# Ten of 22 row groups multiplied by h at once on VectorE and summed row by row on ScalarE

## The reference

```python
indices = jnp.take_along_axis(all_indices, pk, axis=-1)
de = down_embed[indices]
ue = up_embed[indices]
z = jnp.einsum('btd,bthkd->bthk', h, de)
z = act(z * jax.nn.softmax(sc, axis=-1))          # act is silu
out = jnp.einsum('bthk,bthkd->btd', z, ue)
```

## Time and profile before

| | |
|---|---|
| median of 3 runs | 3196.2 us |
| lowest and highest | 3188.67 and 3196.66 us |
| span of the profiled execution, first to last instruction | 3168.2 us |
| VectorE busy | 2783.2 us, 88% |
| TensorE busy (matmuls) | 2818.4 us, 89% |
| ScalarE busy | 2105.8 us, 66% |
| POOL busy | 2098.0 us, 66% |
| DMA bytes moved | 856.45 MB |

### The profile page before, as it was taken

How to read it: one execution, slowest core, us unless ns; L and a number is a source line. 1 busy time by engine, 2 the same in 40 slices (tenths; PEclk the granted TensorE clock), 3 DMA queues, 4 the chain that set the end, 5 groups by cost and what they waited for, 6 DMA issues and landing times.

```text
span 3168.2 us, 39919 instructions
## 1 busy us (share of the span) xinstructions
PE 2818.4 (89%) x9216; PEld 1501.1 (47%) x9216; DVE 2783.2 (88%) x10160; ACT 2105.8 (66%) x6641; POOL 2098.0 (66%) x2056
## 2 busy tenths in 40 slices
PE   7998999999899999999999999899899999998963
PEld 4444455545454545444445444444445454444431
DVE  3488999999989899999999899898999999898987
ACT  4476766767776667776666677666676666677642
POOL 0067666677667677666667767667766666766676
PEclk9999999999999999999999999999999999999986
DMA  8078888888888788888888888888888888888888
GB/s 289 16 265 277 276 270 269 274 283 289 275 270 267 261 282 293 279 281 269 269 275 300 263 277 280 265 268 291 270 278 275 271 275 290 282 279 275 269 296 280
DMA packets 189837, 856.45 MB, mean 270 GB/s; under 512 B 36192, under 2 KB 39392, under 8 KB 189088
## 3 DMA queue, kind: packets, MB, share of 16 engines
q0 software_dynamic: 163840, 805.44, 76.5%
q1 hardware_dynamic: 19104, 34.87, 3.2%
q10 hardware_dynamic: 6656, 13.60, 1.2%
HBM read 845.38 MB, written 8.39 MB: 269 GB/s over the span
## 4 chain that ended last, share of the span: by engine, by line
PE 57%; POOL 11%; DVE 10%; DMA 10%; ACT 6%; issue 6%; SPq 0%; DVEq 0%; ACTq 0%; POOLq 0%
PE bank L465 14%; POOL ring L279 11%; DMA ring<-embed,idx 10%; PE bank L508 8%; PE bank L362 7%; PE bank L481 6%; PE bank L342 5%; DVE bank L1166 4%; PE bank L496 4%; PE bank L444 3%; PE bank L371 3%; ACT xc L691 3%; DVE ring L1152 2%; PE bank L472 2%; ACT raw L688 1%
## 5 line engine op out<-in xcount | busy, mean ns | idle before, releaser
L279 POOL DMA_INDIRECT ring<-embed,idx x2048 | 2096.7, 1024 | 1057.9 <-issue 544.3
L1166 DVE SCALAR_TENSOR_TENSOR bank<-ring,coef,bank 128x512 f32<-128x512 f32 x1312 | 990.8, 755 | 7.4 <-issue 0.2
L1152 DVE SCALAR_TENSOR_TENSOR ring<-ring,hcur 128x256 f32<-128x256 f32 x2048 | 827.1, 423 | 185.7 <-DMA ring<-embed,idx 182.6
L508 PE MATMUL bank<-ring,diag_c 128*128 128x512 f32 x1344 | 668.8, 628 | 119.6 <-ACT diag_c L666 103.9
L657 ACT ACTIVATE coef<-prob,zp 128x1 f32<-128x1 f32 x2048 | 459.1, 293 | 456.1 <-DVE ring L1152 454.9
L465 PE MATMUL bank<-w_up,zs 128*128 128x512 f32 x1024 | 490.4, 630 | 69.2 <-ACT zs L779 65.8
L508 PEld LDWEIGHTS bank<-ring,diag_c 128*128 128x128 f32 x1344 | 246.6, 199 | 385.8 <-issue 224.9
L465 PEld LDWEIGHTS bank<-w_up,zs 128*128 128x128 f32 x1024 | 200.7, 201 | 329.7 <-issue 238.6
L997 DVE SCALAR_TENSOR_TENSOR xc<-raw,taps,xc 128x128 f32<-128x128 f32 x960 | 266.0, 351 | 53.8 <-ACT xc L691 53.8
L342 PE MATMUL bank<-w_in,ut 128*128 128x512 f32 (+1 forms) x768 | 285.1, 524 | 4.4 <-ACT seg L679 4.3
L666 ACT ACTIVATE diag_c<-cst,coef 128x128 f32<-128x128 f32 x672 | 234.8, 394 | 49.4 <-PE bank L508 38.9
(11 more groups left out here) (147 smaller groups left out, 3685.1 us busy)
## 6 DMA issues: line engine op xcount, KB each, us to landing
ring<-embed,idx POOLq DMA_INDIRECT x2048, 4.6
ring<-uT SPq DMA_DIRECT2D x4, 2048.0 KB, 14.3
ut<-uT SPq DMA_DIRECT2D x32, 256.0 KB, 6.5
zs<-u SPq DMA_DIRECT2D x32, 256.0 KB, 5.7
out<-acc SPq DMA_DIRECT2D x32, 256.0 KB, 4.7
w_up<-W_upT ACTq DMA_DIRECT2D x1, 4096.0 KB, 12.7
w_in<-W_in ACTq DMA_DIRECT2D x1, 2560.0 KB, 17.0
w_in<-W_in ACTq DMA_DIRECT2D x1, 2048.0 KB, 21.5
```

Source lines behind the costliest of these rows:

```text
L279: pool.indirect_dma_start(out=ring[:, k % RING, :], out_offset=None, in_=embed, in_offset=bass.IndirectOffsetOnAxis(ap=idx[:, half, k:k + ...
L508: m = pe.matmul(bank[SUM][:, :], diag_c[:, (len(PE_ROWS) * t + n) % DIAGS, :], ring[:, k % RING, DP:ROW], start=(n == 0), stop=(n == len(P ...
L1152: m = dve.scalar_tensor_tensor(out=ring[:, k % RING, 0:DP], in0=ring[:, k % RING, 0:DP], scalar=1.0, in1=hcur[:, :], op0=ALU.mult, op1=ALU ...
L1166: dve.scalar_tensor_tensor(out=total if n == len(DVE_ROWS) - 1 else running[:, :], in0=ring[:, k % RING, DP:ROW], scalar=coef[:, k:k + 1], ...
```

## The change

In the ten groups 3, 5, 7, 8, 9, 10, 11, 13, 16 and 19 (`SUMMED`; five of three picks, five of four) VectorE no longer makes a dot for each pick. It waits until all picks of the group have landed and multiplies all of their first 256 numbers by h in one tensor_tensor (768 or 1024 elements), in place in the ring; the weighs of the group two before follow behind it. ScalarE then runs over each product with the probability as its scale and writes the sum of the scaled products to `zp` (a Copy with `accum_out`), waits for its last sum, and makes one silu for all columns of the group in place of one a pick. The other twelve groups stay as they are.

```diff
--- before.py
+++ after.py
@@ -67,6 +67,8 @@
 PE_GRPS = [g for g in range(NGRP) if "P" in GROUPS[g]]
 NPG = len(PE_GRPS)
 assert FIRST[NGRP] == PICKS and FIRST[NEW] < RING
+SUMMED = (3, 5, 7, 8, 9, 10, 11, 13, 16, 19)
+assert all(FIRST[g] % RING < (FIRST[g + 1] - 1) % RING for g in SUMMED)
 
 
 def signal_of(k):
@@ -209,6 +211,7 @@
         cur_ok, conv_ok, cbm_ok, xdt_ok, g_ok, xdec_ok, yoff_ok, y_half, y_ok, dcy_ok, st_ok, rr_ok, bn_ok, x1_ok, h_ok = (
             sem(n) for n in ("cur_ok", "conv_ok", "cbm_ok", "xdt_ok", "g_ok", "xdec_ok", "yoff_ok", "y_half", "y_ok",
                              "dcy_ok", "st_ok", "rr_ok", "bn_ok", "x1_ok", "h_ok"))
+        zp_ok = sem("zp_ok")
         top1_ok, found_ok, pair_ok, top2_ok, pick_ok, ixy_ok, idx_ok, soft_ok, dot_ok, row_used, sum_ok, r2_ok, o_ok = (
             sem(n) for n in ("top1_ok", "found_ok", "pair_ok", "top2_ok", "pick_ok", "ixy_ok", "idx_ok", "soft_ok", "dot_ok",
                              "row_used", "sum_ok", "r2_ok", "o_ok"))
@@ -653,8 +656,16 @@
                 if g == 0:
                     act.wait_ge(soft_ok, 4 * t + 4)
                 act.wait_ge(dot_ok, NGRP * t + g + 1)
-                for k in range(FIRST[g], FIRST[g + 1]):
-                    m = act.activation(coef[:, k:k + 1], prob_v[:, k:k + 1], ACT.Silu, scale=zp[:, k:k + 1])
+                if g in SUMMED:
+                    for k in range(FIRST[g], FIRST[g + 1]):
+                        m = act.activation(ring[:, k % RING, 0:DP], ring[:, k % RING, 0:DP], ACT.Copy,
+                                           scale=prob_v[:, k:k + 1], accum_out=zp[:, k:k + 1])
+                    m.then_inc(zp_ok, 1)
+                    act.wait_ge(zp_ok, len(SUMMED) * t + SUMMED.index(g) + 1)
+                    m = act.activation(coef[:, FIRST[g]:FIRST[g + 1]], zp[:, FIRST[g]:FIRST[g + 1]], ACT.Silu)
+                else:
+                    for k in range(FIRST[g], FIRST[g + 1]):
+                        m = act.activation(coef[:, k:k + 1], prob_v[:, k:k + 1], ACT.Silu, scale=zp[:, k:k + 1])
                 m.then_inc(coef_ok, 1)
                 mine = rows_of(g, "P")
                 if mine:
@@ -1154,6 +1165,14 @@
                 if last:
                     m.then_inc(dot_ok, 1)
 
+            def products(t, g):
+
+                lo, hi = FIRST[g], FIRST[g + 1]
+                for k in range(lo, hi):
+                    dve.wait_ge(row_in[k % RING], 16 * (uses(k) * t + k // RING + 1))
+                of = ring[:, lo % RING:lo % RING + hi - lo, 0:DP]
+                dve.tensor_tensor(of, of, hcur[:, :].unsqueeze(1).to_broadcast([P, hi - lo, DP]), ALU.mult).then_inc(dot_ok, 1)
+
             def weigh(t, k, first):
 
                 n = DVE_ROWS.index(k)
@@ -1183,8 +1202,10 @@
                 if g == 0:
                     dve.wait_ge(hcur_ok, t + 1)
                     dve.wait_ge(soft_ok, 4 * t + 4)
+                if g in SUMMED:
+                    products(t, g)
                 for n in range(max(len(mine), len(late))):
-                    if n < len(mine):
+                    if n < len(mine) and g not in SUMMED:
                         dot(t, mine[n], n == len(mine) - 1)
                     if n < len(late):
                         if n == 0:
```

## The result

The change makes the kernel slower: 3348.9 us (3344.9 to 3354.2, four runs) against 3194.4, a ratio of 1.0495 (95% interval 1.0476 to 1.0515). The span of the profiled execution grew from 3168.2 to 3343.1 us, by 174.9 us; that is more than the 154 of the medians, as the profiled execution before was quicker than the timed ones. The forecast was 3303, by 3.4 us a tile. From one profiled execution to the other the tile lost 5.0 us in the mean, and the end behind the last tile 20.

A forecast was written before the change was run, and what follows sets the result against it. The bound was taken as a chain through ScalarE ahead of the up projection, TensorE and gathers, not VectorE's queue. 0.2 + 1.4 + 1.0 + 0.8 = 3.4 us a tile, 105 us, plus 2, gave span 3275; with 28, 3303 (3190 to 3385).

The forecast's parts named there:

- The direction: Whole kernel: slower, chance 0.75, against 0.07 for the same and 0.18 for faster.
- (a): Group 3: its product waits for the third row and ScalarE's longer group uses up its wait; 0.2 us a tile.
- (b): Group 5 on ScalarE between the copies ahead of the up projection: nothing covers its sums; +1.40 us a tile.
- (d): Group 16: four sums ahead of four diagonals delay the gather needing its first row; +0.8 us a tile.
- (c): Groups 7 to 13: 7 to 11 free on ScalarE; blocking at 11 and 13 reaches TensorE's turns, 1.0 us a tile.
- the end: Groups after the last tile: some 2 us more in all.
- VectorE's gain: VectorE sheds 2.1 us a tile, 67 us over 32 tiles, into waits for rows; nothing subtracted from the forecast.
- VectorE's total work: Faster rival: VectorE's queue sets the pace, so 2.1 us a tile come off, 65 us, to 3131; chance 0.18.
- Only the front: Rival: only (a) and (b) count, with cheaper sums, some 1.3 us a tile, 40 us, to 3236; chance 0.16.
- The gathers: Rival: POOL's gathers starting under VectorE's products wait them out, net +2.4 us of POOL a tile; chance 0.13.

The follow-up runs named there:

- rowwise: The change with all its sums kept on ScalarE, but VectorE multiplying row by row in turn with the weighs; ratio to the kernel before 1.029.
- blocked_dots: The kernel before, with VectorE in the ten groups awaiting all rows and making all dots ahead of the weighs; silus unchanged; ratio 1.0432.
- before_5_late: The kernel before with group 5's silus moved behind the two copies that the up projection waits for; 3158.9 us, ratio 0.9923.
- only5: The change with only group 5 multiplied at once and summed on ScalarE, the others as before; ratio to the kernel before 1.0168.
- rowwise_7to10: The kernel before with only groups 7 to 10 summed on ScalarE, multiplied row by row in turn with the weighs; ratio 1.0023.
- only_7to10: The change with only groups 7, 8, 9 and 10 multiplied at once and summed, the others as before; ratio to the kernel before 1.0154.

## Why the forecast came out as it did

The direction was right, and so were the steps of ScalarE: (a), (b) and (d) were given 2.4 us a tile, 74 us, and `rowwise` lost 93. Blocking was not: (c) and the end were given 33 us, and `blocked_dots` lost 137. That the whole came out no further off than 46 us is in part luck, since the two cover each other by 76 us, and a second error hid 22 (the sum, below).

(a) **Group 3.** 0.2 us forecast. Between the next pick 0 and the next residual the change adds 0.40 us (3.85 late against 3.45), `blocked_dots` 0.47 and `rowwise` -0.25. So it is the product that waits for its third row, on VectorE, ahead of the residual:

```profile
1573.70 0.96 DVE L1174 TENSOR_TENSOR ring<-ring,hcur 128x768 f32<-128x768 f32 x1 [0.92 <-DMA ring<-embed,idx]
```

ScalarE's longer group 3, which the forecast put first, was covered: its wait of 1.32 us before group 4 shrank to 0.30 at 1580.87 and was not used up.

(b) **Group 5 in front of the projection.** 1.40 forecast, 1.17 measured (first copies 3.83 late, copy for the projection 5.00). The sum was over-priced, 0.60 for 0.49, because the accumulator's read overlaps. `before_5_late` shows the place, since it takes 0.55 us from there and the kernel gains 24 us; 31 x 0.55 is 17 of them. What this step left out is the clock. Granted clock (the column behind POOL's) in the seven us from the projection's start, in two tiles of before, two of after:

```profile
1516.00:1523.00 7.00, 6.57 (x12) 2.84 (x13) 7.00 (x25) 3.37 (x11) 5.31 (x6) 0.76 0.84 268
...
1705.00:1712.00 7.00, 6.83 (x16) 3.10 (x17) 7.00 (x27) 3.21 (x12) 5.22 (x6) 1.00 0.79 242
```

```profile
1591.00:1598.00 7.00, 6.62 (x12) 2.89 (x13) 6.40 (x18) 5.04 (x18) 5.48 (x6) 0.76 0.87 276
1689.00:1696.00 7.00, 6.97 (x9) 2.92 (x10) 6.89 (x18) 3.69 (x14) 4.51 (x4) 0.56 0.88 302
```

By single microseconds the granted clock in three of these stretches is half the full one for a time and then full, as in the first and the last: before, 0.50 from 1517 to 1520 and 1.00 from 1521 on; after, 0.50 from 1689 to 1695 and 1.00 from 1696 on. So 0.76 is half rate for about half of the 7 us, 0.56 for some 6. TensorE had idled 2.2 us ahead of the projection before, and 3.3 after. The first 16 matmuls, from the start of the first to that of the seventeenth, take 7.4 us at full rate, most often 9.1 otherwise, and 10.1 to 10.5 in 12 of the 32 tiles after, in none before; over the tiles the mean was 8.4 us before, 9.0 after, 9.3 in `only5`, and 7.4 in `before_5_late`, where 31 of the 32 tiles are at full rate. Over all profiles it goes with the wait ahead: with 1.6 us of it (four kernels) 30 or 31 of 32 tiles took 7.4 us; with 2.2 us (seven kernels) 9 to 26, and none over 10; with 3.3 us (`only5`, `rowwise` and the change) 1 to 10, and 8 to 18 over 10. So behind 1.1 us more of waiting came about 0.6 us more of slow matmuls, in `only5` 0.9. That fits the surplus of `only5`: 1.2 + 0.9 by 31 is 65 us, its profiled execution had 68 from tile to tile, and the timed runs 53.

(c) **Groups 7 to 13.** This is the step that was mis-sized: "Groups 7 to 11 stand between copies and silus of the up projection, where ScalarE waits for TensorE anyway: nothing." True of ScalarE, as `rowwise_7to10` shows (1.0023), and no answer for the ring, as `only_7to10` shows (1.0154). The turns of x came 2.16 us late in place of 1.0, 0.91 of it already at the key scores. Both medians hold some of the clock of (b). In ten of the table's 24 tiles after, the first 16 matmuls took over 10 us; there TensorE waits 0.52 us for L1081, as before, and the key scores are late by the clock alone. In the seven at full clock it waits 1.97 us for L1081, and the turns stand at 44.83 where such tiles of before have 41.70: 3.1 us by blocking, three times the forecast. The forecast followed the weighs of group 11 into POOL's 4.39 us of slack and took the slack for untouched by the groups ahead. With several blocked groups in a row each lateness is handed on through the ring to the next group's gathers: those of picks 21, 32, 39 and 45, which had run through, now wait 1.5, 1.2, 1.9 and 3.3 us for weighs, and the one that had the slack, pick 52, 0.34 where it had waited 3.81 (medians). The weighs of a blocked group, 0.78 us each and not 0.66, add 0.4 to 0.5 us a group to it.

(d) **Group 16.** 0.8 forecast, 1.3 measured (next pick 0 3.45 late, of which 2.16 had come at the turns). By the same subtraction it is 2.7 in `rowwise` and 0.55 in `blocked_dots`. Where TensorE waited 1.36 us for the diagonals it now waits 2.69, and POOL, which ran through, waits for it:

TensorE's timeline after, at the turns of x and at group 16.

```profile
1636.25 1.06 PE L382 MATMUL bank<-cst,xc 128*128 128x128 f32 x8 [1.43 <-ACT seg L738]
...
1645.34 3.70 PE L511 MATMUL bank<-ring,diag_c 128*128 128x512 f32 x8 [2.69 <-ACT diag_c L677]
```

POOL's timeline after, at the gather that needs a row of group 16.

```profile
1649.31 0.97 POOL L282 DMA_INDIRECT ring<-embed,idx  x1 [2.90 <-PE bank L511]
```

**The end behind the last tile.** 2 us forecast, 19.9 measured. There nothing but the groups is left, so the ring's loop is the whole path: 17.9 us with blocking alone, 3.2 with ScalarE alone.

**VectorE's gain.** 12.1 less 10.0 us a tile were forecast to end in waits, 67 us of busy time less; 19.7 came off. The products were priced well (1610.27 to 1611.42 is 1.15 us for 1.13); but 19 weighs a tile now start right behind another one, 5 before, and the 0.12 us that each loses come to 54 us (14 x 32 x 0.12). The waits for landings grew by 238. Nothing of the gain reached the end: right.

**The sum.** 5.0 us by 31 intervals are 154, with 20 at the end 174, the span's 174.9. The forecast of the span was low by 68 us. Of that 22 were hidden by a second error: the median before lies 28 us above the profiled span, and the text ahead of the prediction put that ahead of the first and behind the last instruction; but the profiled execution after took 3344.9 us for its span of 3343.1, so what lies around a span is 1.8 us. By the medians, 154 us apart with the end included, a tile would lose some 4.3 us.

**The rivals.** VectorE's total work did not set the pace of the tile: it was relieved and the tile got longer. The order of its queue did. "Only the front" is `only5`, a third of the loss. The gathers were wrong as a cause. No run shows the 2.4 us a tile that were worked out for them, left out of the sum and taken in by the upper end of the forecast's range:

POOL's gathers after, from the groups by line: count, busy us, mean ns, idle.

```profile
L282 POOL DMA_INDIRECT ring<-embed,idx x2048 | 2063.9, 1008 | 1263.5 <-issue 498.4 <-PE bank L511 321.9 <-DVE bank L1185 277.7
```

1008 ns a gather in place of 1024 (2096.7 us busy before). More gathers are stretched, 99 of over 1.3 us in place of 72, but by less in total: POOL is busy for 1.0 us a tile less, where that estimate had 2.4 more. Gathers that start under a product do stretch more often than others, one to 1.58 us at 1603.41 under the product of 1603.21: of the 99 that start under one 43 took over 1.3 us, of the other 1949 only 56. Before, it was 31 of the 37 that start under the multiplication of 2048 elements, and 41 of the other 2011. So the stretch exists and its price did not count. What holds such a gather up, no run shows.

## What to carry to other kernels

An instruction that takes several rows at once also takes the latest row's landing, for itself and for all that is queued behind it; where the queue behind it frees the buffers that the next loads wait for, that is a loop, and in a ring of 13 slots it cost 4.3% with no more work on any engine. Price such a change by the wait at the group's last row and by who is freed late, not by busy time, and don't call a place covered on one engine before the other queues through it were looked at. In front of a TensorE stretch, a wait that grows can also go with a lower clock behind it: here, behind 1.6 us of waiting the first 16 matmuls took the 7.4 us of the full clock in 30 or 31 of 32 tiles, and behind 3.3 us in 1 to 10. Moving three silus out of that place gave 0.8%.

## What the runs showed of the hardware

Two things were not expected. The read of ScalarE's accumulator in the kernel after, 0.19 to 0.26 us busy, held the queue for only 0.09 us when another sum followed, and for 0.20 to 0.29 us, 0.22 at the median, at a group's last sum, where ScalarE waits for it. And the granted clock behind a wait of TensorE was not the same from tile to tile at the same place: over the 7 us from the projection's start 1.00 or 0.76 behind 2.2 us of waiting in the kernel before, 0.55 to 0.61 in 12 of the 32 tiles after, behind 3.3 us, and 1.00 from the second tile on in `before_5_late`, behind 1.6 us. What decides between these tiles is left open; no run varied the wait by itself.
